# Cross-attention kernel: the set-up in another order, with the value projection behind group 0's scores

## The reference

```python
q = _split_heads(hidden_states @ w_q, HEADS)
k = _split_heads(text @ w_k, HEADS)
v = _split_heads(text @ w_v, HEADS)
out_text = _merge_heads(_sdpa(q, k, v))
k_ip = _split_heads(ip_h @ w_k_ip, HEADS)
v_ip = _split_heads(ip_h @ w_v_ip, HEADS)
out_ip = _merge_heads(_sdpa(q, k_ip, v_ip, mask=mask_ip))   # mask from 4 boxes on a 32 x 32 grid
out = (out_text + IP_SCALE * out_ip) @ w_out + b_out + residual
```

## Time before and its profile

| | |
|---|---|
| median of 3 runs | 923.88 us (923.59 to 924.72) |
| the profiled execution | 924.26 us, of which its span is 922.5 us |
| PE busy | 890.0 us, 96% of the span |
| DVE / ACT / POOL busy | 727.3 / 605.6 / 524.2 us |

### The profile page before, as it was taken

How to read it: one execution, slowest core, us unless ns; L and a number is a source line. 1 busy time by engine, 2 the same in 40 slices (tenths; PEclk the granted TensorE clock), 3 DMA queues, 4 the chain that set the end, 5 groups by cost and what they waited for, 6 DMA issues and landing times.

```text
span 922.5 us, 13827 instructions
## 1 busy us (share of the span) xinstructions
PE 890.0 (96%) x4685; PEld 753.1 (82%) x4685; DVE 727.3 (79%) x999; ACT 605.6 (66%) x982; POOL 524.2 (57%) x422
## 2 busy tenths in 40 slices
PE   7999879999999999999999999999999999999968
PEld 7977758888888888888888888888888888888846
DVE  6484888888797978887887979787887879797772
ACT  5464767675848577675858486775768485866651
POOL 3372637466473929375664839284756648392731
PEclk9999999999999999999999999999999999999979
DMA  8685020303030110303030301203030303010001
GB/s 266 221 272 170 22 71 2 122 1 129 1 122 1 58 70 2 119 0 128 0 121 0 127 1 47 73 0 128 0 121 0 128 0 112 1 58 1 38 20 58
DMA packets 34151, 64.79 MB, mean 70 GB/s; under 512 B 4428, under 2 KB 6604, under 8 KB 33996
## 3 DMA queue, kind: packets, MB, share of 16 engines
q1 hardware_dynamic: 32812, 61.82, 19.7%
q10 hardware_dynamic: 1312, 2.62, 1.0%
HBM read 40.84 MB, written 23.59 MB: 70 GB/s over the span
## 4 chain that ended last, share of the span: by engine, by line
PE 82%; DVE 4%; ACT 1%; POOL 1%; issue 1%; POOLq 0%; DVEq 0%
PE bank L105 22%; PE bank L107 22%; PE bank L106 22%; PE bank L874 7%; PE bank L883 4%; PE bank L884 4%; DVE total L765 1%; DVE o_raw L754 1%; DVE pT_lo L747 1%; POOL prob L552 1%; DVE prob L552 0%; ACT oT_hi L672 0%; POOL prob L558 0%; DVE prob L558 0%; DVE top L759 0%
## 5 line engine op out<-in xcount | busy, mean ns | idle before, releaser
L619 POOL TENSOR_TENSOR oT_lo<-o_raw,oT_hi 128x512 fp32r<-128x512 f32 x80 | 103.0, 1288 | 254.0 <-ACT oT_hi L672 254.0
L558 POOL TENSOR_TENSOR prob<-prob,inv 128x1120 f32<-128x1120 f32 x124 | 169.7, 1401 | 8.6 <-DVE inv L767 8.6
L552 POOL TENSOR_TENSOR prob<-prob,top 128x1120 f32<-128x1120 f32 x124 | 174.3, 1435 | 0.0
L105 PE MATMUL bank<-xT_hi,wq_hi 128*128 128x512 f32 x400 | 162.2, 406 | 2.6 <-DVE qT_lo L137 2.6
L105 PE MATMUL bank<-oT_hi,wo_hi 128*128 128x512 f32 x400 | 158.1, 395 | 0.9 <-POOL oT_lo L619 0.6
L107 PE MATMUL bank<-oT_hi,wo_lo 128*128 128x512 f32 x400 | 157.9, 395 | 0.0
L106 PE MATMUL bank<-oT_lo,wo_hi 128*128 128x512 f32 x400 | 157.8, 394 | 0.0
L107 PE MATMUL bank<-xT_hi,wq_lo 128*128 128x512 f32 x400 | 156.9, 392 | 0.0
L106 PE MATMUL bank<-xT_lo,wq_hi 128*128 128x512 f32 x400 | 156.3, 391 | 0.0
L754 DVE TENSOR_TENSOR o_raw<-bank,pv_part 64x512 f32<-64x512 f32 x160 | 110.2, 689 | 48.6 <-ACT pv_part L668 44.6
L759 DVE TENSOR_REDUCE top<-prob 128x20 f32<-128x1120 f32 (+1 forms) x128 | 98.7, 815 | 43.9 <-POOL prob L607 43.7
(11 more groups left out here) (88 smaller groups left out, 1740.3 us busy)
## 6 DMA issues: line engine op xcount, KB each, us to landing
outT<-res SPq DMA_DIRECT2D x80, 256.0 KB, 6.8
xin<-in_xT SPq DMA_DIRECT2D x14, 1280.0 KB, 6.9
w_raw<-in_L_xattn_w_v SPq DMA_DIRECT2D x8, 320.0 KB, 4.8
w_raw<-in_L_xattn_w_k SPq DMA_DIRECT2D x8, 320.0 KB, 3.7
w_raw<-in_L_xattn_w_v_ip SPq DMA_DIRECT2D x8, 320.0 KB, 3.8
w_raw<-in_L_xattn_w_k_ip SPq DMA_DIRECT2D x8, 320.0 KB, 3.8
xin<-in_xT ACTq DMA_DIRECT2D x2, 1280.0 KB, 8.1
v_raw<-v_scratch SPq DMA_DIRECT2D x16, 160.0 KB, 4.4
```

The costliest lines, as they stand in the source:

```text
L105: nc.tensor.matmul(dst, a_hi, b_hi, start=first, stop=False)
L552: ins = eng.tensor_tensor(s, s, top[:, t, n, :].unsqueeze(2).broadcast_to([P, HEADS, k1 - k0]), ALU.subtract)
L558: ins = eng.tensor_tensor(s, s, inv[:, t, n, :].unsqueeze(2).broadcast_to([P, HEADS, k1 - k0]), ALU.mult)
L619: nc.gpsimd.tensor_tensor(oT_lo[:, m, :], o_raw[:, m % 2, :], oT_hi[:, m, :].bitcast(F32), ALU.subtract).then_inc(oT_lo_done, 1)
```

## The change

1. The set-up's order becomes: text keys and ip keys for 8 slices, group 0's queries, group 0's scores, and then ip values and text values for 8 slices, while ACT, DVE and POOL do group 0's softmax between the value chunks. Then two query tiles of group 1. All of this is in the first block; group 0 enters the second block at its transposes.
2. Group 0 then leaves three query tiles of group 1 for between its pairs, as all other groups do; its residuals move there too.
3. Text values are made in four blocks of 128 tokens (448 = 3 x 128 + 64), each cut into 416 and 224 columns. The last block's 64 tokens stand beside their own remainders (`tails`), so that it needs two matmuls in place of three, and two partition halves are added afterwards. The ip projections for keys and for values are separate, each of 512 and 128 columns.
4. Value chunks have a ring of 5 places laid over `wo_hi` and `wo_lo`; `w_raw` has 7 slots; group 0's first keys and values no longer pass through DRAM (`k_all` and `v_text` are read directly).
5. `LINE = 64`, and a tile `grid` of 128 bytes behind `inv`: the tiles laid behind `k_raw` now start at 128 modulo 512. `ctxT` holds hi and lo of a slice beside each other, 3584 bytes for a slice.
6. `make_mask` moves behind group 0's `k_lo`. The last group shares its softmax with DVE as before; group 0 no longer does.

```diff
-LINE = 32
+LINE = 64
 RING = 4
-LOADS = 6
+LOADS = 7
+WRING = 5
+Q_AHEAD = 2
...
+            with ExitStack() as context:
+                ctxT = sb("ctxT", [P, KC, 2, TT], F32R, context)
+            ctxT_hi, ctxT_lo = ctxT[:, :, 0, :], ctxT[:, :, 1, :]
...
             for k in range(KC):
-                stream("v", k)
+                chunks += [("k", k), ("k_ip", k)] if k < KC - 1 else [("k_ip", k), ("k", k)]
+                chunks += [("q", n) for n in {KC - 3: (0,), KC - 2: (1, 2), KC - 1: (3, 4)}.get(k, ())]
             for k in range(KC):
...
+                chunks += [("v_ip", k), ("v", k)]
...
+            WIDE, NARROW = 416, D - 416
+
+            def v_pieces(i):
+                b0 = 3 * (i // 2)
+                if i % 2 == 0:
+                    return (b0, 0, 0, WIDE), (b0 + 1, 0, WIDE, D)
+                return (b0 + 1, NARROW, 0, NARROW), (b0 + 2, 0, NARROW, D)
...
+                    for h in range(2):
+                        sp.dma_start(v_raw[h * KEYS:h * KEYS + NTEXT, :], v_text[0:NTEXT, 0, :]).then_inc(v_raw_loaded, 16)
+                        sp.dma_start(v_raw[h * KEYS + NTEXT:(h + 1) * KEYS, :], v_ip[0:NIP, :]).then_inc(v_raw_loaded, 16)
+                    sp.dma_start(v_ip_scratch, v_ip[:]).then_inc(v_stored, 16)
+                    sp.wait_ge(v_text_act, 2)
+                    sp.wait_ge(v_text_dve, 6)
+                    sp.dma_start(v_scratch[0:(BLOCKS - 1) * P, :].rearrange("(i p) d -> p i d", p=P), v_text[:, 0:BLOCKS - 1, :]).then_inc(v_stored, 16)
+                    sp.dma_start(v_scratch[(BLOCKS - 1) * P:TT, :], v_text[0:TAIL, BLOCKS - 1, :]).then_inc(v_stored, 16)
+                    sp.wait_ge(v_raw_loaded, 64)
+                    sp.wait_ge(v_stored, 48)
...
+                    for t in range(3):
+                        add_mask(pool, 0, t)
+                    sub_max(pool, 0, 0, 1)
+                    add_mask(pool, 0, 3)
+                    sub_max(pool, 0, 1, 1)
+                    lo_chunk(behind[0])
+                    sub_max(pool, 0, 2, 1)
+                    lo_chunk(behind[1])
+                    sub_max(pool, 0, 3, 1)
+                    lo_chunk(behind[2])
+                    normalise(pool, 0, 0, 0, 1)
+                    lo_chunk(behind[3])
+                    normalise(pool, 0, 1, 0, 1)
+                    for c in behind[4:]:
+                        lo_chunk(c)
+                    normalise(pool, 0, 2, 0, 1)
+                    normalise(pool, 0, 3, 0, 1)
...
+                    q_lo_part(dve, 0, 0)
+                    k_lo_part(dve, 0, k_all[:, 0, :, :])
+                    make_mask()
...
+                    for m in range(1, KD):
+                        q_lo_part(dve, 0, m)
+                        if m <= len(ahead):
+                            lo_chunk(ahead[m - 1])
+                    for t in range(GT):
+                        maxima(dve, 0, t)
+                    lo_chunk(behind[0])
+                    sums(dve, 0, 0, 0)
+                    lo_chunk(behind[1])
+                    sums(dve, 0, 1, 1)
+                    for k in range(KD):
+                        x_lo_part(dve, 1, 1, k)
+                    sums(dve, 0, 2, 2)
+                    lo_chunk(behind[2])
+                    sums(dve, 0, 3, 3)
...
+                    for n in range(UNITS):
+                        score_unit(pe, 0, n, 0, True)
+                    for k in range(KC):
+                        if k == 0:
+                            pe.wait_ge(q_lo_done, KD)
+                        ip_tokens("v_ip", k, V_IP_BANKS, value_w_used, v_ip_ready)
+                        text_values(k)
+                    pe.wait_ge(v_ip_added, len(V_IP_BANKS))
+                    for m in range(Q_AHEAD):
+                        q_steps(pe, 1, m)
```

More of the change, by code:

```diff
@@ new lines, in score_unit @@
+        def score_unit(pe, g, n, b, new_batch):
+            if n < 2:
+                wait(pe, score_copied, UNITS * g)
+            elif n < 4:
+                wait(pe, pT_lo_done, PAIRS * g)
+            else:
+                pe.wait_ge(score_copied, UNITS * g + n - 3)
+            if n == 0 and new_batch:
+                pe.wait_ge(k_built, HPT * (b + 1))
+            for half in range(2):
+                t, m = divmod(2 * n + half, KD)
+                if t == 0:
+                    pe.wait_ge(q_lo_done, KD * g + m + 1)
+                q_cols = slice(t * P, (t + 1) * P)
+                keys = [k[:, m, :, :].rearrange("p j k -> p (j k)") for k in (k_hi, k_lo)]
+                ins = three(s_bank[n % 4][:, half * CW:(half + 1) * CW], qT_hi[:, m, q_cols], qT_lo[:, m, q_cols], *keys, True, True)
+            ins.then_inc(score_ready, 1)
@@ new lines, in _ @@
+                    behind = [c for c in mine if V0 + WRING <= c < WO0]
+                    for m in range(1, KD):
+                        q_lo_part(dve, 0, m)
[7 more added lines that the diff above has]
+                    sums(dve, 0, 1, 1)
@@ L470, in _, with ip_tokens @@
-                    ins.then_inc(k_ipT_ready, 1)
+                            ins.then_inc(key_w_used, 1)
+                    def ip_tokens(name, k, banks, used, ready):
+                        wait_lo(pe, name, k)
+                        toks = ipT_parts[:, k, :, :].rearrange("p s t -> p (s t)")
+                        for n, (i, c0, c1) in enumerate(banks):
+                            for part, w in enumerate(place(name, k)):
+                                ins = nc.tensor.matmul(bank[i][:, 0:c1 - c0], toks, w[:, c0:c1], start=k == 0 and part == 0, stop=k == KC - 1 and part == 1)
+                            if k == KC - 1:
+                                ins.then_inc(ready, 1)
+                        if k < KC - 1:
+                            ins.then_inc(used, 1)
@@ L685, in v_hi_part, with softmax @@
                         nc.scalar.activation(v_head(v_parts, 0, j), v_own(j), ACT.Copy).then_inc(v_hi_built, 1)
-                def group(g, u, b, before, more, shared=0):
+                def softmax(g, u, b, more, shared=0):
                     def split_x(k0, k1):
@@ L717, in group, with values @@
                     if more:
-                        for m in range(0 if before else 3, q_ahead(before)):
+                        for m in range(Q_AHEAD):
                             q_hi_part(act, g + 1, m)
+                def values(g, u, b, more, residuals=()):
                     pT_part(g, 0)
@@ L818, in group, with values @@
                     if more:
-                        for m in range(0 if before else 3, q_ahead(before)):
+                        for m in range(Q_AHEAD):
                             q_lo_part(dve, g + 1, m)
+                def values(g, more):
                     pT_part(g, 0)
@@ L916, in group @@
                         if more:
-                            for m, k in q_slot(s, before):
+                            for m, k in q_slot(s):
                                 if k == 0:
```

729 lines of the change are left out of this document (374 added, 355 removed).

## The result

The changed kernel takes **921.51 us** in the median of its runs; the kernel before takes 923.5 us beside it. The ratio is 0.9976, with a 95% interval of 0.9969 to 0.9982. The forecast was 910.4 us with a range of 904 to 920, so it had the sign but not the size, and the time lies outside the range.

What follows compares the result with a forecast made beforehand. The prediction took PE as the bound, busy 96% of the span. Set-up -7.0 us and placing -6.5 gave -13.5 on the profiled 924.26: 910.8, or 910.4 us against the median, range 904 to 920.

Steps and rivals of the forecast that it cites:

- keys: Key stage of the set-up: DMA lets the queries begin at 39.5 us, against 38.2 for PE alone; lost 1.3 us.
- queries: Group 0's queries: the mask on DVE delays `q_lo` of tile 1, so PE waits; lost 2.4 us.
- scores: Group 0's scores: with the last `q_lo` a bit late, lost 0.7 us, as before.
- values: Values under group 0's softmax: value-chunk remainders queue behind softmax work on DVE and POOL; lost 3.2 us.
- two query tiles and the change of block: End of the first block: stores and `q_lo` of tile 1 end late, then the block change; lost 3.0 us.
- group 0's pairs: New block: POOL's and DVE's preparation costs 0.6 us and ACT's residuals 1.2; lost 1.8, where 9.8 was lost before.
- The forecast's own sign of failure: Value stage: the forecast is wrong if a chunk's wait repeats with every slice, or the group length does not move.
- Narrow matmuls: Set-up's value and ip matmuls of 224 and 128 columns: taken at 0.108 us each, expected at 0.105 to 0.12.
- The dear-matmul rival: Set-up's narrow fp32r matmuls run below full rate, making the run slower: 925 to 952 us, chance 0.08.
- Placing: Later groups and keys: moving operands at 128 modulo 512 shorten matmul distances; 6.5 us gained, bounds 0 and 8.
- The likeliest case: Whole kernel: set-up gains 7.0 us and placing 6.5, both within their bounds; 905 to 916 us, chance 0.57.
- the second rival, "the set-up gives nothing": Set-up: late chunks delay each other, and slower DMA (+2) and stores (+3) return 5 or 6 us; 917 to 920, chance 0.15.

Runs made afterwards that it cites:

- x parts late: Changed kernel with group 0's x parts 0 and 1 made behind chunk q3, no longer ahead of slice 7's tokens: 920.06 us, kernel before 924.06.
- mask in idle time: Changed kernel with make_mask on DVE directly ahead of `q_lo` of tile 0, where DVE idles, not behind `k_lo`: 920.03 us, kernel before 923.87.
- three orders: Changed kernel with `q_lo` first, mask in idle time and x parts late, no edit in the values: 913.73 us, kernel before 923.89.
- `q_lo` first: Changed kernel with DVE's second value-chunk remainder moved behind the last query remainder (`q_lo` of tile 4): 918.01 us, kernel before 924.18.
- output chunks behind: x last, with DVE's two output chunks' remainders moved behind its evacuation of the value banks: 910.10 us, kernel before 923.70.
- Place only: Kernel before with LINE = 64 and nothing else: 918.08 us against 924.18, ratio 0.9930.
- the pad: Kernel before with an unused 128-byte tile ahead of `oT_hi`, moving `oT` and what follows: 917.61 us against 924.18, one run.
- round ahead: Changed kernel with ACT rounding each value chunk one place earlier, ahead of the exponential: 924.44 us, kernel before 924.06.
- x last: Changed kernel with `q_lo` first, mask in idle time, x parts late, round ahead, and group 1's x remainders behind DVE's last value chunk: 913.76 us, ratio 0.9885.
- POOL kept quiet: Output chunks behind, with POOL also waiting for the ip additions before normalising tiles 2 and 3: 908.84 us, kernel before 923.77.
- set-up-only kernel: Changed kernel with LINE = 32, the old placing, and nothing else: 927.91 us, kernel before 924.18, ratio 1.0041.

## Why the prediction was wrong, step by step

The forecast's account, and the same account of the changed kernel (PE's time in a stage less its matmuls at their undisturbed distances; the columns differ from the 10.5 us between 133 and 143.5 by 0.3):

| term | forecast | measured |
|---|---|---|
| start | 8.4 | 8.8 |
| keys | 1.3 | 4.9 |
| queries | 2.4 | 2.9 |
| scores | 0.7 | 2.2 |
| values | 3.2 | 6.6 |
| two query tiles and the change of block | 3.0 | 2.9 |
| group 0's pairs | 1.8 | 3.3 |
| sum | 20.8 | 31.6 |

- **Keys: the step failed.** It asked when DMA brings the chunks, and took DMA as the bound at 39.5 (10.3 MB at 339 GB/s are 30.4 us, not 31). Queries start at 43.5, with the queries' weights and x there; DMA is busy 0.77 in 34 to 44. What was not followed is DVE's own queue in the last slices: 2.2 + 2.65 us of remainders for the queries ahead of slice 7's tokens, a gap of 2.6 us on PE, and nine matmuls at the lower clock, 1.7 us. By the rows at 37.90 and 39.98 DVE's 4.9 us would be some 2.1 without POOL beside it (an estimate). A smaller wait for tokens at 31.78 costs 0.4, and `ctxT` 0.3: its matmuls take 0.2065 in five slices instead of 0.203, where the forecast had them gain 0.003. With x parts late and mask in idle time (three orders) the queries start at 39.97, so 39.5 was not far from what DMA allows.
- **Scores: the step failed.** "With the last `q_lo` a bit late: lost 0.7, as before" was copied from the kernel before. In the new order a value chunk stands on DVE ahead of `q_lo` of tiles 3 and 4, and its rounding on ACT behind `q_hi` of tile 4. `q_lo` first, a change of two lines, took the loss to 0.2 and the run down by 3.5, 2.0 of it in this stage.
- **Values: mis-sized; the wait was the one foretold.** The wait for a text chunk's remainder behind sums and x was foretold at 3.2 us, and came at 2.0. Not in the sum were the waits for three ip chunks from POOL (0.8, 0.6 and 0.4), the lower clock behind the gap (1.7 us; the window 94 to 98 has the clock at 0.65), and 0.1 us more a slice than the matmuls' sum. The lower clock is no loss of its own here, since with `q_lo` first the stage is as long at the full clock: the chain of chunks and softmax on ACT, DVE and POOL sets its 37.78 us. The forecast's own sign of failure, that a chunk's wait repeats with later slices, did occur in part.
- **Pairs: mis-sized**, 3.3 against 1.8. The gap of the block change was costed, at its right size, but the eight transposes and four query matmuls behind it take 3.4 us, at the lower clock, instead of 1.8. At the full clock (`q_lo` first, output chunks behind) the loss is still 2.4.
- **Queries, the start and the change of block** were near, 0.5, 0.4 and 0.1 us off: PE waits 2.35 us for `qT_lo` behind the mask, forecast 2.4, and 2.9 at the block change, forecast 3.0.
- **Narrow matmuls: right.** 224 columns start 0.11 us apart, 128 columns no more; a value slice with its ip projections takes 4.00 us undisturbed, forecast 3.92. The dear-matmul rival is out.
- **Placing: right in size, in part by luck.** 6.5 us came, 0.43 a group instead of 0.40, but nearly all from `oT`; `pT` gives 0.001 of the 0.002 a matmul, `ctxT` nothing. The forecast's own parts (0.38 and 0.04 a group, 0.36 once) add up to 7.1 us, not to its 6.5; the sum was nearer than its parts. Place only and the pad show that the place of `oT` changes the distance. The rule of the Trainium skill (TensorE: Matmul & The Clock Gate, Back-to-back issue gap), which has no term for an operand's place, does not hold for it.

The likeliest case thus failed in one half: placing gave its 6.5 us, the set-up lost 3.5 instead of gaining 7.0. What came is nearest to the second rival, "the set-up gives nothing", given 917 to 920 and 0.15. Its cause was right, DVE and POOL serving softmax and remainders in turn, with every late chunk delaying the next. Its two prices were not. DMA at the lower rate (+2) did not hold the queries, which start at 39.97 with three orders, and the stores (+3) did not hold the block change, which cost 2.9 us as in the main forecast. The losses above the forecast, 10.8 us, stand in the keys, scores, values and pairs instead, and the time lies above that rival's range too. The reason "each chain was followed with measured durations" did not carry: they were durations of instructions that stood alone, and in two of the five stages, the keys and the scores, the chain was not followed at all.

The experiments show the cause to be these orders and not the order of the stages as such. With six moves (`q_lo` first, mask in idle, x parts late, round ahead, x last, output chunks behind) and no work taken away, group 1 starts at 131.73 and the run takes 910.1 us; with POOL kept quiet 908.84. That 910.1 is the forecast's number is chance, since it is another kernel and its terms are others. What stays open: the pairs' remaining 2.4 us, and why some gaps are followed by the lower clock and others not (below).

## What to carry to other kernels

Follow the in-order queue of every helper engine through each stage, also where a stage "is as before", and price a gap on PE by its length plus what the clock rows show behind such gaps. Work that nobody waits for yet (x of the next group, output weights, the last normalisings) belongs behind the last item that PE does wait for, and POOL left idle beside DVE's long subtractions was worth more than POOL kept at work (910.1 to 908.84 us). Judge an edit by the stage that it changes, not only by the total: two edits gave 2.7 us each in their stages and 0.6 and 1.1 us at group 1, because the clock behind a gap elsewhere differed in that execution.

## What the runs showed of the hardware

- A matmul of 512 columns starts 0.2271 us behind the last when its moving operand `oT` begins at 128 modulo 512, and 0.2324 when it begins at 0. For `ctxT`, 448 columns, no such rule comes out: 0.2065 in five slices of the changed kernel and 0.202 in a sixth, with hi and lo at 128 and 384 in all of them; 0.200 in the set-up-only kernel (0 and 256); 0.203 both in the kernel before (0 or 256) and with place only (128 or 384). So the place of `oT` is shown, and that 128 is better for every operand is not.
- Subtractions on DVE with both inputs in SBUF (128x512, fp32r out) take 0.62 to 0.67 us with POOL idle part of the time, and 1.6 to 1.9 beside a POOL that works through (five in 3.1 to 3.3 against 8.2 to 9.4 us). Sums on DVE beside the same POOL work kept their 0.78 us each. Beside them POOL slows too: four normalisings take 6.7 us, 4.9 in the earlier trace rows. 8.75 us for five is 1.75 each, and 6.73 for four is 1.68 each, near one of DVE's own 0.62 and one of POOL's 1.23 in turn, 1.85. The Trainium skill (SBUF — State Buffer, Who interferes with whom) says that a DVE instruction with two SBUF inputs contends with a GpSimd instruction that reads SBUF, and calls this contention an exclusive lock; these rows agree, with near to one whole POOL instruction added to each of DVE's. The forecast allowed "up to twice" for the parts of x; it was 2.7 times, and it did not let DVE's delay feed back.
- A PE gap of 2.6 us in the keys, of 2.1 in the values and of 3.2 at the block change each had matmuls at the lower clock level behind it, nine in the keys; the gap of 2.7 in the queries and that of 2.0 ahead of the scores did not (granted clock 1.00 in both windows). Length alone does not decide. Between kernels the same gap goes either way: the 2.7 us in the queries are followed by the lower level with x parts late (0.92 in that window), the 3.1 us at the block change by the upper level in `q_lo` first (1.00), where the changed kernel has 0.67 in the first 5 us. The runs do not tell what decides.
